# First layer of a two-layer attention kernel: output chain of a batch moved on by whole groups, four mask buffers, both slots' first rows written together

## What is computed

```python
def _L0_xattn_ref(x, mask, kv, kv_mask, Wq, bq, Wk, bk, Wv, bv):        # 8 batches, 256 channels, 512 positions
    q = einsum('oc,bct->bot', Wq, x) + bq;  k, v = the same of kv with Wk, Wv
    ...                                                                  # 16 heads of 16 channels
    attn = softmax(where(kv_mask, q * scale @ k, -inf))
    mean = attn @ v;  ex2 = attn @ (v * v)
    std = sqrt(relu(ex2 - mean * mean))
    xn = _masked_instance_norm(x, mask)                                  # per row of 512: masked mean and variance
    return (xn * std + mean) * mask
def _L1_xattn_ref(hidden_states, ...):                                   # on the result as 256 tokens of 512
    x = x + self-attention(layernorm(x));  x = x + cross-attention(layernorm(x), ctx)
    return x + gelu(layernorm(x) @ w1 + b1) @ w2 + b2
```

## The kernel before

| function | engine | line | where before (w % 4, step) | waits for |
|---|---|---|---|---|
| `finish_shares` (`mean_a`, `second`) | GpSimd | L914 | 3, between the regroups | `rz` by DMA |
| `mean_squared` | ScalarE | L843 | 3, step 6 | `mean_a` |
| `finish_variance` (`std_a`) | GpSimd | L914 | 3, after the second regroup | L843 |
| `positive_variance` | VectorE | L684 | 0, step 2 | `std_a` |
| `roots` | ScalarE | L848, L849 | 0, step 3 | L684 |
| `normal_x` | VectorE | L688, L691 | 0, step 6 | `roots` |
| `finish_x` | GpSimd | L914 | 0, last | L691 |
| `last_mask` | VectorE | L697 to L703 | 1, steps 5 and 6 | `finish_x` |

## Time and profile before

### The profile page before, as it was taken

How to read it: one execution, slowest core, us unless ns; L and a number is a source line. 1 busy time by engine, 2 the same in 40 slices (tenths; PEclk the granted TensorE clock), 3 DMA queues, 4 the chain that set the end, 5 groups by cost and what they waited for, 6 DMA issues and landing times.

```text
span 1758.6 us, 30853 instructions
## 1 busy us (share of the span) xinstructions
PE 1644.4 (94%) x10578; PEld 1133.5 (64%) x10578; DVE 1261.0 (72%) x2758; ACT 1061.1 (60%) x2351; POOL 516.4 (29%) x795
## 2 busy tenths in 40 slices
PE   6899989899898988999999999999999899999999
PEld 3333334343343345788878777888888788888888
DVE  2677878788787737998999889999999762323222
ACT  1465767667666657787877878788887741121111
POOL 0134555546445442332223222222232220000000
PEclk8799999999998998999999999999999899999999
DMA  4555355463543513233232534333333330000000
GB/s 155 162 172 170 104 154 142 143 187 107 148 130 117 160 49 86 66 78 76 66 95 74 144 81 116 91 92 92 92 90 81 97 114 1 25 0 25 0 25 13
DMA packets 112619, 167.97 MB, mean 96 GB/s; under 512 B 27464, under 2 KB 43208, under 8 KB 112336
## 3 DMA queue, kind: packets, MB, share of 16 engines
q1 hardware_dynamic: 88580, 132.15, 25.8%
q0 software_dynamic: 20992, 29.12, 6.8%
q10 hardware_dynamic: 2892, 4.72, 1.0%
HBM read 72.06 MB, written 34.60 MB: 61 GB/s over the span
## 4 chain that ended last, share of the span: by engine, by line
PE 57%; DVE 20%; ACT 7%; issue 6%; DMA 5%; SPq 3%; POOL 2%; ACTq 0%; DVEq 0%; POOLq 0%
PE ps L543 11%; PE ps L1951 9%; PE ps L1925 7%; PE ps L520 5%; DVE at_t L1403 4%; PE ps L1274 4%; DVE at_t L1408 4%; PE ps L1284 4%; PE ps L529 3%; PE ps L497 2%; PE ps L1223 2%; DMA rz<-shares 2%; PE ps L1930 2%; PE ps L1212 2%; ACT at_prob L1611 2%
## 5 line engine op out<-in xcount | busy, mean ns | idle before, releaser
L623 DVE TENSOR_REDUCE nmax<-ps 128x2 f32<-128x1024 f32 x256 | 310.5, 1221 | 139.2 <-PE ps L520 138.1
L788 ACT ACTIVATE prob<-ps 128x1024 f32<-128x1024 f32 x256 | 261.6, 1022 | 158.4 <-PE ps L529 154.1
L1611 ACT ACTIVATE at_prob<-at_t,at_nmax 128x256 f32<-128x256 f32 x512 | 256.6, 506 | 86.5 <-DVE at_nmax L1408 75.4
L543 PE MATMUL ps<-prob,v 128*64 128x512 f32 x1024 | 275.1, 630 | 0.2
L1408 DVE CUSTOM_DVE_ANT_0 at_t<-at_t,at_off 128x256 f32<-128x256 f32 x512 | 233.6, 493 | 8.8
L1769 POOL TENSOR_TENSOR at_low<-at_low,at_high 128x512 fp32r<-128x512 f32 x64 | 86.7, 1355 | 462.1 <-DVE at_high L1437 462.1
L2110 DVE CAST mlp_h_hi<-mlp_h 128x512 fp32r<-128x512 f32 x64 | 28.4, 444 | 212.9 <-ACT mlp_h L2022 179.9
L520 PEld LDWEIGHTS ps<-ring 64*128 64x128 f32 x512 | 49.5, 190 | 185.3 <-issue 133.9
L2022 ACT ACTIVATE mlp_h<-ps,b 128x512 f32<-128x512 f32 x48 | 33.1, 690 | 218.3 <-PE ps L1925 218.3
L1223 PE MATMUL ps<-ident,at_prob 128*128 128x128 f32 x1024 | 158.9, 278 | 0.0
L520 PE MATMUL ps<-ring 64*128 64x512 f32 x512 | 132.4, 514 | 22.3 <-DMA ring<-rows 10.0
(11 more groups left out here) (218 smaller groups left out, 3929.7 us busy)
## 6 DMA issues: line engine op xcount, KB each, us to landing
ring<-rows SPq DMA_DIRECT2D x62, 512.0 KB, 6.3
rows<-shares_of SPq DMA_DIRECT2D x90, 256.0 KB
at_k_stack<-at_high SPq DMA_DIRECT2D x256, 64.0 KB, 2.5
at_q_stack<-at_high SPq DMA_DIRECT2D x128, 64.0 KB, 2.7
at_q_stack<-at_high POOLq DMA_DIRECT2D x128, 64.0 KB, 2.4
at_q_stack<-at_low SPq DMA_DIRECT2D x128, 64.0 KB, 2.1
at_k_stack<-at_low POOLq DMA_DIRECT2D x128, 64.0 KB, 2.4
c_in<-in_ctx SPq DMA_DIRECT2D x8, 512.0 KB, 9.1
```

The lines of the kernel that those rows point to most:

```text
L543: mm = eng.matmul(ps[2 * QD * k:2 * QD * (k + 1), VB, :], v[:, c, HG * G + 2 * p + k, :], prob[:, M % PROBS, k, :], start=(c == 0), stop=( ...
L623: eng.tensor_reduce(nmax[:, n % 2, j, 2 * p:2 * p + 2], ps[:, at:at + 2, :], AX, ALU.max, negate=True).then_inc(s_max, 1)
L788: eng.activation(prob[:, M % PROBS, :, :], ps[:, ST:ST + 2, :], ACT.Exp, scale=float(HD0) ** -0.5).then_inc(s_exp, 1)
L1611: ins = eng.activation(prob[:, m % 2, i, :], t[:, p, i, :], ACT.Exp, scale=-1.0, bias=nmax[:, m % 4, i:i + 1], accum_out=z[:, T % 2, j, 2 ...
```

## The change

For the batches of the steady part, the functions of the table move: `finish_shares` behind the second regroup of group 3; `mean_squared` to group 0, step 1; `finish_variance` on GpSimd between the two regroups of group 0; `positive_variance` to group 0, step 5; `roots` to group 1, step 5; `normal_x` to group 1, step 7; `finish_x` between the two regroups of group 2; `last_mask` to group 2, steps 6 and 7. For batch 6 (`LAST - 1`) they stand at the seam: `mean_squared` in w = 32, step 1; `positive_variance`, `roots` and `normal_x` in steps 3, 4 and 6 (before 2, 3 and 5); `last_mask` in w = 33, steps 4 and 5 (before 2 and 3); `finish_variance` and `finish_x` behind GpSimd's loop. There are four mask buffers in place of three, in other places of memory, and all uses take b % 4.

At the start, the constants and the first rows of slots 0 and 1 go out in the same DMAs: q's on ScalarE's queue, k's on SyncE's. SyncE has no second round of them: four constant DMAs and six row DMAs fewer. `written` and `constants_written` count accordingly; `high_of` for the second q waits for the first writes alone.

The three places of `variances` and `inverse_roots` for the second layer's first norms move from steps -47, -46, -41, -40 to -37, -35, -34, -33 (counted from w = 32).

```diff
--- before.py
+++ after.py
@@ -128,16 +128,16 @@
-        mask = [None, sb("mask1", [P, D]), None]
+        mask = [None, None, None, sb("mask3", [P, D])]
         v_out = sb("v_out", [P, OUTS, D])
-        mask[0] = sb("mask0", [P, D])
+        mask[2] = sb("mask2", [P, D])
...
@@ -252,7 +253,8 @@
             eng.wait_ge(s_first_out[name], 3 * DMA)
-            eng.wait_ge(s_out[name], 3 * DMA * (m + 1))
+            if m:
+                eng.wait_ge(s_out[name], 3 * DMA * m)
...
@@ -324,11 +326,11 @@
-            constants_out(1, far, s_far_out, 0, RING if b else 1)
-
-        def rows_out(name, m, slots=(0, 1)):
-
-            k, at = "qk".index(name), slice(2 * m % RING + slots[0], 2 * m % RING + slots[-1] + 1)
+            constants_out(1, far, s_far_out, 0, RING if b else 2)
+
+        def rows_out(name, m):
+
+            k, at = "qk".index(name), slice(2 * m % RING, 2 * m % RING + 2)
...
@@ -382,19 +382,15 @@
         eng.wait_ge(s_one, 1)
-        constants_out(0, scrap, s_const, 0, 1)
+        constants_out(0, scrap, s_const, 0, 2)
         far_out(0)
-        rows_out("k", 0, (0,))
+        rows_out("k", 0)
         for p in range(2):
             first_rows_in("k", p)
         for p in range(2):
             first_rows_in("q", p)
         eng.dma_start(w0[:, :, 2 * S:], d["w0"][:, :, 2 * S:]).then_inc(s_wv, DMA)
         eng.dma_start(bv0[:], d["bv0"]).then_inc(s_wv, DMA)
-        constants_out(0, scrap, s_const, 1, 2)
-        constants_out(1, far, s_far_out, 1, 2)
-        rows_out("k", 0, (1,))
-        rows_out("q", 0, (1,))
         rows_in("k", 1)
         rows_in("q", 1)
         constants_out(0, scrap, s_const, 2, RING)
...
@@ -739,12 +735,14 @@
-                if w % NG == 0 and 0 <= b - 2 < LAST and s == 2:
+                if w % NG == 0 and 0 <= b - 2 < LAST and s == (5 if w < GROUPS else 3):
                     positive_variance(b - 2)
-                if w % NG == 0 and 0 <= b - 2 < LAST and s == (6 if w < GROUPS else 5):
+                if w % NG == 1 and 0 <= b - 2 < LAST - 1 and s == 7 or (w, s) == (GROUPS, 6):
                     normal_x(b - 2)
-                if w % NG == 1 and 0 <= b - 2 < LAST and s in ((5, 6) if w < GROUPS else (2, 3)):
-                    last_mask(b - 2, (s + 1) % 3)
+                if w % NG == 2 and 0 <= b - 2 < LAST - 1 and s in (6, 7):
+                    last_mask(b - 2, s - 6)
+                if w == GROUPS + 1 and s in (4, 5):
+                    last_mask(b - 2, s - 4)
                 lead(w, s)
...
@@ -791,13 +789,13 @@
             eng.wait_ge(s_bits if b else s_first_bits, DMA)
-            if b >= 3:
-                eng.wait_ge(s_masked, SB * (b - 2))
-            eng.activation(mask[b % 3][:], m_in[:, b, :], ACT.Copy).then_inc(s_mask, 1)
+            if b >= 4:
+                eng.wait_ge(s_masked, SB * (b - 3))
+            eng.activation(mask[b % 4][:], m_in[:, b, :], ACT.Copy).then_inc(s_mask, 1)
...
@@ -863,8 +861,8 @@
         for part, at in ((0, 0), (0, 48), (1, 16)):
-            eng.dma_start(d["rows0"][0, 0:1].rearrange("s p (i r) t -> (s p i) r t", r=ROWS)[:, at:at + HD0, :],
-                          shares_of[0:ROWS, 0, part, :].bitcast(F32)).then_inc(s_first_out["q"], DMA)
+            eng.dma_start(d["rows0"][0, 0:2].rearrange("s p (i r) t -> (s p i) r t", r=ROWS)[:, at:at + HD0, :],
+                          shares_of[:, 0, part, :].bitcast(F32)).then_inc(s_first_out["q"], DMA)
...
@@ -886,9 +884,9 @@
-                if s == 6 and w % NG == 3 and 0 <= b - 1 < LAST:
-                    mean_squared(b - 1)
-                if s == 3 and w % NG == 0 and 0 <= b - 2 < LAST:
+                if s == 1 and w % NG == 0 and 0 <= b - 2 < LAST:
+                    mean_squared(b - 2)
+                if s == 5 and w % NG == 1 and 0 <= b - 2 < LAST - 1 or (w, s) == (GROUPS, 4):
                     roots(b - 2)
                 lead(w, s)
...
@@ -943,22 +941,21 @@
             if n >= 0:
                 regroup(eng, 2 * n)
-            if w % NG == 3 and 0 <= b - 1 < LAST:
-                finish_shares(b - 1, 0)
-                finish_shares(b - 1, 1)
-            if n >= 0 and w % NG == 3:
-                regroup(eng, 2 * n + 1)
-            if w % NG == 3 and 0 <= b - 1 < LAST:
-                finish_variance(b - 1)
+            if w % NG == 0 and 0 <= b - 2:
+                finish_variance(b - 2)
             if w % NG == 0 and 0 < b < NB:
                 squares(2 * b)
             if w % NG == 2 and b < NB:
                 squares(2 * b + 1)
-            if n >= 0 and w % NG < 3:
-                regroup(eng, 2 * n + 1)
-            if w % NG == 0 and 0 <= b - 2:
+            if w % NG == 2 and 0 <= b - 2:
                 finish_x(b - 2, 0)
                 finish_x(b - 2, 1)
+            if n >= 0:
+                regroup(eng, 2 * n + 1)
+            if w % NG == 3 and 0 <= b - 1 < LAST:
+                finish_shares(b - 1, 0)
+                finish_shares(b - 1, 1)
+        finish_variance(LAST - 1)
         finish_x(LAST - 1, 0)
         finish_x(LAST - 1, 1)
```

More of the change, by code:

```diff
@@ L139, in layer0 @@
         far = sb("far", [P, D])
-        mask[2] = sb("mask2", [P, D])
+        mask[0] = sb("mask0", [P, D])
         ring = sb("ring", [P, RING, 4, D], F32R)
@@ L157, in layer0 @@
         loaded = sb("loaded", [P, 1])
+        mask[1] = sb("mask1", [P, D])
         x_hi, x_lo, c_hi, c_lo, w_hi0 = (g[name + "0"] for name in ("x_hi", "x_lo", "c_hi", "c_lo", "w_hi"))
@@ L339, in rows_out @@
                     eng.wait_ge(s_ring[name][n % RING], loads_of(n) * DMA)
-            src = shares_of[ROWS * slots[0]:ROWS * (slots[-1] + 1), k, :, :]
             for part, row in ((0, 0), (0, 48), (1, 16)) if name == "q" else ((0, 0), (0, 16), (1, 48)):
                 eng.dma_start(d["rows0"][k, at].rearrange("s p (i r) t -> (s p i) r t", r=ROWS)[:, row:row + HD0, :],
-                              src[:, part, :].bitcast(F32))\
-                   .then_inc((s_first_out if m == 0 and slots == (0,) else s_out)[name], DMA)
+                              shares_of[:, k, part, :].bitcast(F32)).then_inc((s_out if m else s_first_out)[name], DMA)
         def constants_written(name, n):
             if name == "q":
-                eng.wait_ge(s_const, 2 * DMA * min(n + 1, 3))
+                eng.wait_ge(s_const, 2 * DMA * (1 if n < 2 else 2))
             else:
-                eng.wait_ge(s_far_out, 2 * DMA * (n // NG + min(n + 1, 3)))
+                eng.wait_ge(s_far_out, 2 * DMA * (n // NG + (1 if n < 2 else 2)))
         def first_rows_in(name, p):
@@ L652, in masked_x @@
                 made(eng, "q", 2 * b + 1)
-                eng.tensor_reduce(cnt[:, b, 0:1], mask[b % 3][:], AX, ALU.add)
-            eng.tensor_tensor_reduce(X[:, b, h, :], X[:, b, h, :], mask[b % 3][:], 1.0, 0.0, ALU.mult, ALU.add,
+                eng.tensor_reduce(cnt[:, b, 0:1], mask[b % 4][:], AX, ALU.add)
+            eng.tensor_tensor_reduce(X[:, b, h, :], X[:, b, h, :], mask[b % 4][:], 1.0, 0.0, ALU.mult, ALU.add,
                                      sums[:, b, 0, h:h + 1]).then_inc(links.sem, 1)
@@ L659, in squares_of_x @@
             if b == 0 and h == 0:
-                eng.wait_ge(s_const, 6 * DMA)
+                eng.wait_ge(s_const, 4 * DMA)
             eng.tensor_tensor_reduce(scrap[:], X[:, b, h, :], X[:, b, h, :], 1.0, 0.0,
@@ L696, in last_mask @@
             eng.wait_ge(s_fin, FINISH * (b + 1))
-            eng.tensor_tensor(X[:, b, h, :], X[:, b, h, :], mask[b % 3][:], ALU.mult).then_inc(s_masked, 1)
+            eng.tensor_tensor(X[:, b, h, :], X[:, b, h, :], mask[b % 4][:], ALU.mult).then_inc(s_masked, 1)
             eng.wait_ge(s_masked, SB * b + h + 1)
@@ L793, in masks @@
             eng.wait_ge(s_bits if b else s_first_bits, DMA)
-            if b >= 3:
-                eng.wait_ge(s_masked, SB * (b - 2))
-            eng.activation(mask[b % 3][:], m_in[:, b, :], ACT.Copy).then_inc(s_mask, 1)
+            if b >= 4:
+                eng.wait_ge(s_masked, SB * (b - 3))
+            eng.activation(mask[b % 4][:], m_in[:, b, :], ACT.Copy).then_inc(s_mask, 1)
             if b:
-                eng.wait_ge(s_far_out, 2 * DMA * (b + 2))
+                eng.wait_ge(s_far_out, 2 * DMA * (b + 1))
             eng.wait_ge(s_mask, b + 1)
-            eng.activation(far[:], mask[b % 3][:], ACT.Identity, bias=row[:, FAR_OFF:FAR_OFF + 1],
+            eng.activation(far[:], mask[b % 4][:], ACT.Identity, bias=row[:, FAR_OFF:FAR_OFF + 1],
                            scale=row[:, FAR_AT:FAR_AT + 1]).then_inc(s_far, 1)
@@ L1496, in lead @@
             step = 8 * (w - G0) + s
-            if step == -47:
+            if step == -37:
                 variances(0)
-            if step in (-46, -41, -40):
-                inverse_roots(0, (-46, -41, -40).index(step) + 1)
+            if step in (-35, -34, -33):
+                inverse_roots(0, (-35, -34, -33).index(step) + 1)
             if step == -6:
```

## The result

| | before | changed |
|---|---|---|
| median of 20 runs each | 1746.8 us | 1755.6 us |
| lowest to highest | 1740.6 to 1755.0 | 1747.6 to 1767.0 |
| profiled execution, its span | 1760.4, 1758.6 | 1751.2, 1749.4 |

The ratio is 1.0055, with a 95% interval of 1.0039 to 1.0072: the change costs 8.8 us by the medians and 9.6 by the ratio. Medians and ratios in this document leave out executions that took over 1.5% more than the fastest of the same kernel; among them are two of 1767 us at an ordinary clock in the second measurement of the changed kernel, and with them its median is 1754.8 us and not 1752.3. The forecast was 1738 us, in a range of 1720 to 1752. By the two profiled executions alone the changed kernel is 9.2 us faster.

The account below looks back on a forecast made before the run. TensorE, busy 503.6 of 538 us, sets the pace, so only its stalls can be won back. The terms sum to -12.4, taken as -13: 1760.4 profiled becomes 1747.7, scaled to 1738 us; range 1720 to 1752.

Parts of the forecast that it names:

- Start, -5.5: Kernel start: writing both slots at once ends a 3.56 us wait, with clock and earlier tops: -3.6 -1.2 -1.0 +0.3.
- The price in front: Kernel start: first writes of 256 KB instead of 128 take the same 9 us, larger constants +0.3; bounds 0 and +9.
- The rival of slow first writes, +9: Kernel start: first writes stay at 83 GB/s, costing +9 us, so 1747 us; chance 0.10.
- The part on the clock: Kernel start: the k product may run at twice the clock once the idle stretch goes: -1.9, of which -1.2 taken.
- Batch start, -17.2: Batch starts: moving mean_squared later ends TensorE's waits, 8.7 us, and low clock there, 8.5 us.
- The scaling, 1750.9/1760.4: Whole kernel: the profiled execution's forecast of 1747.7 us, scaled by median over profiled time, gives 1738 us.
- Regroup traffic, +2.1: Batch's last group: GpSimd's second regroup, now earlier, falls among the ring's loads on full DMA: 0.35 us, six times.
- Roots, +2.2: Group 1, step 5: TensorE's wait for the roots becomes 2.4 us against 2.03, six times; low clock left as is.
- `mean_squared`, +1.8: Batch's first group, step 1: mean_squared follows two evictions, costing 0.3 us a batch; between 0 and 6.4 in all.
- the last mask, +0: Group 2, steps 6 and 7: moving last_mask there from group 1 costs nothing; upper bound +6 if GpSimd is late.
- the slower rival: Group 2: VectorE waits at last_mask for GpSimd's finish_x, delaying maxima and TensorE; 1769 us; chance 0.09.
- Last groups, +4.2, with 1.9 lost in it: Second layer's start: GpSimd's finish_x starts at 634.9 instead of 630.72, and TensorE's 1.9 us lead is lost; bounds +2, +7.

Follow-up runs that it names:

- head_only: Kernel before with only both slots' first rows, constants and far rows written together, output chain left where it was: 1742.1 us, ratio 0.9962.
- shares_first: Changed kernel with GpSimd's finish_shares put back before the second regroup of a batch's last group: 1743.5 us, ratio 0.9978 to the kernel before.
- the pair without tables: head_only and shares_first, each with copies for the square roots of batches 0 to 5: 1722.0 us (0.9864) and 1720.8 us (0.9857).
- after_small_pool: Changed kernel with GpSimd's multiplications and additions of the output chain on 32 columns in place of 512: 1739.1 us, ratio 0.9951 to the kernel before.
- head_small_pool: head_only with GpSimd's multiplications and additions of the output chain on 32 columns in place of 512: 1722.5 us, ratio 0.9861 to the kernel before.
- after_fourth: Changed kernel without an edit, its fourth profiled execution, to set held squares beside time: 1755.9 us, two squares held.

## Why the prediction was wrong, by its own steps

- *Start, -5.5.* Right: -6.7. The wait of 3.56 us in the earlier trace rows is 0.64 now, and the eviction of q is at 36.08, 0.04 us behind its product. The price in front is too small to read: the first maxima come at 27.95 us (27.58 before), but the executions of one kernel differ by more (26.35 in the kernel before's second, 26.49 in the changed kernel's). The rival of slow first writes, +9, is out. The part on the clock holds in most executions: in the changed kernel's first the k product is still at 0.50 (3.62 us), but in 11 of the 16 profiled executions with the new start it takes 2 us at 1.00, as in `head_only`, last row below; with the old start it takes 3.1 to 3.8 in all three.

```profile
38.64 2.05 PE L502 MATMUL ps<-w,c_in 128*128 128x128 f32 x16 [0.64 <-DVE shares_of L612]
...
43.05 3.62 PE L482 MATMUL ps<-c_in,w 128*128 128x512 f32 x4 [1.92 <-DVE v L640]
```
```profile
42.00 1.98 PE L481 MATMUL ps<-c_in,w 128*128 128x512 f32 x4 [1.92 <-DVE v L639]
```

- *Batch start, -17.2.* The mechanism was right, the size was not. The wait behind `mean_squared` went, but it is 4.4 us in the second execution of the kernel before, not 8.7, and none of that execution's low stretches lies there, so the 8.5 of clock were mostly not there to be won. The sign that the forecast named, a count of low stretches that changes by more than two, came at once: four in the first profile of the changed kernel (200.3, 275.4, 487.0 and 565.5), from nine. From `head_only` to `shares_first` the mean clock of the runs rises from 0.976 to 0.978, about 3 us at 1.5 us for 0.001. So 7 to 8 us, and not 17.
- *The scaling, 1750.9/1760.4.* This treated the excess of the profiled execution as spread over everything. Much of it sat in the low-clock stretches, 37.5 us at clock 0.50 against 17 (some 10 us of time at half speed), of which the batch-start term had booked 8.5 as a gain. A saving that is read from an execution's excess can't be booked against a median that doesn't have it.
- *Regroup traffic, +2.1.* The step that failed, beside the size of the batch start. Its sentence, "GpSimd's second regroup of that group now goes ahead of `finish_shares`", was costed as DMA traffic alone: nothing asked which instruction of VectorE lies beside GpSimd's multiplications in their new place. It puts `finish_shares` on the cast and shifts the next batch so that `finish_variance` can meet the squares: 9 to 12 us. Waits for the ring, slots and top rows, grew besides: they are 9.5 us in `shares_first` (5.9 and 3.6) and 4.1 in the second execution of the kernel before. That is one execution against one; the first of the kernel before has 9.3, the five of the changed kernel 5.9 to 13.9, mean 10.3. The moved DMAs are not what brings them, since `shares_first` has them behind `finish_shares` again; what does is open.
- *Roots, +2.2.* Right: 2.37 to 2.42 us in five of six batches, +2.5 to +4 by the pair without tables. The low clock follows them still, as in the kernel before.
- *`mean_squared`, +1.8, and the last mask, +0.* At the first TensorE waits 0.43 us for the exponential behind it, in two of six batches, and 0.18 in one (1.0 us in all); in `shares_first` it is 0.42 to 0.43 in five (2.1). The first of them (timeline of the changed kernel):

```profile
320.10 0.51 PE L525 MATMUL ps<-ring 64*128 64x512 f32 x2 [0.43 <-ACT prob L786]
```

  The forecast had it that `last_mask` cost nothing on TensorE in group 1. It did cost: steps 5 and 6 took 3.48 us each there in the kernel before, and take 2.0 and 2.7 without it in the changed kernel's second execution. In group 2 it makes steps 6 and 7 longer by 2.0 us (2.9 and 3.8 for 2.1 and 2.6). The two nearly cancel, so that the 0 for the move was right by luck. VectorE waits once, 0.9 us, for GpSimd's `finish_x` in group 2: the slower rival's place, but not its price. Even that one wait is what the forecast named as a sign of being wrong. The fear of a loss on VectorE was right in kind and wrong in place; it is no wait on a semaphore, which is why the waits view doesn't show it, but an instruction that runs for 4 us.
- *Last groups, +4.2, with 1.9 lost in it.* The mechanism was right, the size twice too large: +2.2 to +2.3 measured from the last maxima on (56.5 to 58.8 us), just inside the bounds. The roots start 1.5 us later after the last maxima, as forecast. From there to `finish_x` it is 5.0 us (613.91 to 618.88) where the forecast had 6.7: it put the whole block of 3.65 us before the eviction of k, but the eviction stands before the second table load, at 616.26. (Its terms add up to 634.6 and not to 634.9, too.) The idle time of TensorE before its product of k grew from 4.97 to 8.99 us. The chain through the seam, as in the earlier trace rows, and ScalarE's and TensorE's rows:

```profile
618.88 2.49 POOL X L912 x2
```
```profile
616.26 0.82 ACT L1622 ACTIVATE at_low<-ps,b_feat 128x256 f32<-128x256 f32 x2
...
633.44 0.80 PE L1267 MATMUL ps<-at_v,w_raw 128*128 128x256 f32 x1 [8.99 <-ACT at_low L1622]
```

With the measured sizes: start -6.7, batch starts -7 to -8, roots +2.5, waits for the ring +5.4, seam +2.2, held VectorE +9 to +12. That adds up to +4 to +8, some 1752 to 1756 from the 1747.7 of the kernel before. The last term is a difference between whole kernels and the ring's comes from two single executions, so the agreement is no proof of the parts.

## What to carry to other kernels

Moving work on GpSimd can be a change to VectorE too: write down which instruction of VectorE runs beside each of its multiplications in the new place, before counting queues and transfers. Read a stage's low-clock stretches from more than one execution before booking them as a gain, and compare the profiled execution with the median and the mean clock of the runs. A wait that is moved to a later step is paid for where it lands; three places gave TensorE waits of 2.03, 2.4 and 2.8 us for the same instructions.

## What the runs showed of the hardware

Some VectorE instructions beside GpSimd's multiplications are held, and not slowed in proportion: the cast's 0.17 us and the square's 0.68 become 3.9 and 4.6, and they end within 0.1 us of or up to 0.6 us after GpSimd's last one. With 32 columns of GpSimd's work in place of 512 none is held (`after_small_pool`, `head_small_pool`). Not every kind is: maxima, whose input lies in PSUM, take their usual 1.2 us in the middle of a multiplication (timeline of the kernel before, second execution):

```profile
166.91 2.51 POOL L914 TENSOR_TENSOR mean_a<-mean_in,rz 128x512 f32<-128x512 f32 x2 [5.48 <-DMA rz<-shares]
168.08 1.22 DVE L623 TENSOR_REDUCE nmax<-ps 128x2 f32<-128x1024 f32 x1 [1.43 <-PE ps L520]
...
169.40 2.49 POOL L914 TENSOR_TENSOR second<-second,rz 128x512 f32<-128x512 f32 x2
...
169.81 0.89 DVE L633 CAST wide<-nmax 128x16 fp32r<-128x16 f32 x1
170.74 1.19 DVE L635 TENSOR_TENSOR wide<-nmax,wide 128x16 fp32r<-128x16 f32 x1
```

By the Trainium skill, "SBUF — State Buffer", section "SBUF: two separate sides", VectorE and GpSimd share one pair of ports under an exclusive lock for the whole of an instruction, which an operation of VectorE needs only in a two-port mode or with two inputs in SBUF. The maxima and the square agree with it; that the cast runs in a two-port mode no run here shows. The lock for one instruction agrees here, where the cast is let in after 0.89 us, at the end of one multiplication (169.40 + 1.25 = 170.65), and `L635` at the end of the next. It does not cover the changed kernel, where the same cast stays out over three more of them, 3.95 us. What decides between the two is open, and it is not when the cast starts. In the long ones it mostly started 0.2 us before the end of a multiplication (164.06 and 307.76) and in short ones 0.4 (159.59) and 0.8 us (169.81) before it; but a cast that started 0.2 us before the end was also let in at once, with the same order of GpSimd (timeline of `after_fourth`), and in the last group of the first layer one that started 0.95 us before it took 4.67 us, in each of the five executions of the changed kernel (600.15 in the first).

```profile
384.85 2.50 POOL L912 TENSOR_TENSOR mean_a<-mean_in,rz 128x512 f32<-128x512 f32 x2
385.90 0.28 DVE L629 CAST wide<-nmax 128x16 fp32r<-128x16 f32 x1
```
